# First tokens normed tile by tile, last counts between additions, and a graph convolution's matrix scaled a tile ahead

## What is computed

```python
xn = _layernorm(x)
x = x + _L0_gnn_ref(xn, W1, b1, W2, b2, edge_index) + _L0_mix_ref(xn[None], w_map, ...)[0]
# _L0_gnn: twice gcn_conv, A = D^-1/2 (counts of edges + identity) D^-1/2, deg = row sums
#   h = relu(A (xn W1) + b1);  out = A (h W2) + b2
# _L0_mix: linear attention: k, v = layernorm per head (12 heads of 64), att = k^T v / n, out = (q att) w_out
```

## Time and profile before

| | us |
|---|---|
| median of three runs | 2002.79 |
| the profiled execution, its own time | 2000.80 |
| its span, first to last instruction | 1998.9 |
| PE busy | 1862.9 (93%) |
| DVE busy | 1292.3 (65%) |
| ACT busy | 934.8 (47%) |

### The profile page before, as it was taken

The page is one execution under the profiler, slowest core; times in us unless marked ns, Lnnn a source line. Parts: engine busy times, 40 slices in busy tenths (PEclk is TensorE's granted clock), DMA queues, the critical chain, the costliest instruction groups (busy, mean ns, idle before and its releaser), DMA issues.

```text
span 1998.9 us, 30899 instructions
## 1 busy us (share of the span) xinstructions
PE 1862.9 (93%) x12197; PEld 1769.2 (89%) x12198; DVE 1292.3 (65%) x2466; ACT 934.8 (47%) x1543; POOL 154.5 (8%) x129
## 2 busy tenths in 40 slices
PE   5997998899999999788679999999999999999998
PEld 4885788899889999788679999999999999999998
DVE  6997766545345646888873764356565666676886
ACT  2321222324233535878543233336555666666775
POOL 0000000004000003333110000000101001001010
PEclk8997999999999989899889999999999999999999
DMA  3110002101122211110212132255656657676795
GB/s 116 48 48 1 24 25 97 38 24 49 48 72 88 72 38 46 69 38 17 95 51 87 49 103 72 71 187 194 206 202 212 216 213 239 232 259 233 286 327 195
DMA packets 36796, 234.30 MB, mean 117 GB/s; under 512 B 5916, under 2 KB 7318, under 8 KB 14632
## 3 DMA queue, kind: packets, MB, share of 16 engines
q1 hardware_dynamic: 31318, 217.41, 30.4%
q0 software_dynamic: 2656, 8.99, 2.0%
q10 hardware_dynamic: 2674, 5.87, 0.8%
HBM read 221.91 MB, written 10.35 MB: 116 GB/s over the span
## 4 chain that ended last, share of the span: by engine, by line
PE 45%; issue 6%; DVE 3%; ACT 2%; DMA 1%; POOL 0%; ACTq 0%; POOLq 0%; DVEq 0%
PE bank L2682 8%; PE bank L341 7%; PE bank L342 7%; PE bank L343 7%; PE bank L2683 3%; PE bank L2694 3%; PE bank L2698 2%; PE bank L2686 2%; PE bank L2695 2%; PE bank L2697 1%; PE bank L2685 1%; DVE weight_lo L314 1%; PE bank L2643 0%; PE bank L2032 0%; DMA weight_raw_fifth<-in_ffn_w 0%
## 5 line engine op out<-in xcount | busy, mean ns | idle before, releaser
L314 DVE TENSOR_TENSOR weight_lo<-weight_raw,weight_hi 128x2304 fp32r<-128x2304 f32 (+1 forms) x155 | 392.3, 2535 | 46.1 <-ACT weight_hi L304 45.9
L304 ACT ACTIVATE weight_hi<-weight_raw 128x2304 fp32r<-128x2304 f32 (+1 forms) x155 | 323.2, 2087 | 71.4 <-DMA weight_raw<-in_ffn_w 50.8
L341 PE MATMUL bank<-xT_hi,weight_hi 128*128 128x320 f32 (+1 forms) x576 | 182.6, 317 | 1.9 <-DVE xT_lo L362 1.8
L342 PE MATMUL bank<-xT_lo,weight_hi 128*128 128x320 f32 (+1 forms) x576 | 177.8, 309 | 0.0
L343 PE MATMUL bank<-xT_hi,weight_lo 128*128 128x320 f32 (+1 forms) x576 | 177.6, 308 | 0.0
L341 PE MATMUL bank<-weight_hi,xT_hi 128*128 128x384 f32 (+1 forms) x480 | 161.9, 337 | 7.9 <-DVE xT_lo L362 4.5
L3056 DVE TENSOR_TENSOR hidden_tmp<-hidden_tmp,bank 128x160 f32<-128x160 f32 (+5 forms) x192 | 65.7, 342 | 159.1 <-ACT hidden_tmp L2842 159.1
L342 PE MATMUL bank<-weight_lo,xT_hi 128*128 128x384 f32 (+1 forms) x480 | 157.5, 328 | 0.0
L343 PE MATMUL bank<-weight_hi,xT_lo 128*128 128x384 f32 (+1 forms) x480 | 157.3, 328 | 0.0
L665 PE MATMUL bank<-one_hot_dst,one_hot_src 125*128 125x313 f16 x800 | 122.9, 305 | 15.2 <-ACT packed_counts L679 7.9
L2842 ACT ACTIVATE hidden_tmp<-bank,ffn_b_by_load 128x160 f32<-128x160 f32 (+5 forms) x192 | 73.6, 404 | 121.0 <-PE bank L2686 118.8
(11 more groups left out here) (499 smaller groups left out, 5078.9 us busy)
## 6 DMA issues: line engine op xcount, KB each, us to landing
weight_raw<-in_ffn_w SPq DMA_DIRECT2D x111, 1152.0 KB, 5.2
weight_raw_fifth<-in_ffn_w SPq DMA_DIRECT2D x25, 1152.0 KB, 5.3
weight_raw<-in_shared_w SPq DMA_DIRECT2D x16, 1152.0 KB, 5.1
weight_raw<-in_mix_kv SPq DMA_DIRECT2D x8, 1152.0 KB, 5.2
weight_raw<-in_gat_w SPq DMA_DIRECT2D x8, 768.0 KB, 4.2
weight_raw<-in_mix_q SPq DMA_DIRECT2D x4, 1152.0 KB, 5.0
weight_raw<-in_mix_out SPq DMA_DIRECT2D x4, 1152.0 KB
weight_raw<-in_gnn_w SPq DMA_DIRECT2D x4, 1152.0 KB, 5.1
```

What stands on the lines that cost most here:

```text
L304: act.activation(upper_, whole_, ACT.Copy).then_inc(*w_hi.one())
L314: dve.tensor_tensor(lower_, whole_, upper_.bitcast(F32), ALU.subtract).then_inc(*w_lo.one())
L341: pe.matmul(dst, a[0], b[0], start=first, stop=False)
L342: pe.matmul(dst, a[0], b[1], start=False, stop=False)
```

## The change

The first norm uses `tile_norm`: x comes in tiles, each with a semaphore of its own, with weight 0 and the edges between tiles 1 and 2. Tiles 0 and 1 are normed before the first product, tiles 2 to 4 between the first keys' products and the first columns; weight 1 is split after tile 4. In `project(1)` each of the last four unpacking steps follows an addition, and weight 8 is split before `project(1)`. In the graph convolution tile t + 1 is scaled before `adj_lo` of tile t. The hooks `scalar_meanwhile` and `vector_meanwhile` of `layer_norm` go away.

```diff
-        sp.dma_start(x[:, 0:TT - 1, :], ins["x"][0:(TT - 1) * P, :]...).then_inc(*x_in.dma())
-        sp.wait_ge(blank.semaphore, 1)
-        for a0, n in parts_of_16(LAST):
-            sp.dma_start(x[a0:a0 + n, TT - 1, :], ...).then_inc(*x_in.dma())
+        def tile(t):
+            sp.dma_start(x[:, t, :], ins["x"][t * P:(t + 1) * P, :]).then_inc(*x_in[t].dma())
+        tile(0)
+        tile(1)
+        weights_load(1)
         for n, name in enumerate(("src", "dst")):
             for a0, rows in parts_of_16(EP):
                 sp.dma_start(edges_i[a0:a0 + rows, n, :], ins[name][a0:a0 + rows, :]).then_inc(*edges_in_.dma())
+        tile(2)
+        tile(3)
+        sp.wait_ge(blank.semaphore, 1)
+        for a0, n in parts_of_16(LAST):
+            sp.dma_start(x[a0:a0 + n, TT - 1, :], ...).then_inc(*x_in[TT - 1].dma())
         weights_load(DEPTH - 1)
...
             def keys_or_values(n, beside):
                 w = weight("mix0_kv", n)
                 for t in range(TT):
+                    if n == 0:
+                        if 2 <= t + 1 < TT:
+                            norm.turn_tensor(t + 1)
+                        pe.wait_ge(*norm.ready[t])
                     bank = ring.next(kv_copied.at(TT * n + t + 1))
...
-            pe.wait_ge(*xT_ready)
+            pe.wait_ge(constants.semaphore, 2)
+            norm.turn_tensor(0)
+            norm.turn_tensor(1)
             keys_or_values(0, FIRST)
...
+        def moments_of(t):
+            dve.wait_ge(*x_in[t].now())
+            norm.stats_vector(t)
+        def first_vector_steps():
+            moments_of(0)
+            norm.scale_vector(0)
+            moments_of(1)
+            norm.scale_vector(1)
+            norm.lower_vector(0)
+            norm.lower_vector(1)
+            dve.memset(zeros[:, :, :], 0.0).then_inc(*pads_blank.one())
+            edges_ready()
+            return dve_own.now()
...
+            norm.root_scalar(0)
+            norm.root_scalar(1)
+            norm.upper_scalar(0)
+            norm.upper_scalar(1)
+            weight_hi(0)
+            norm.root_scalar(2)
+            norm.upper_scalar(2)
+            act.wait_ge(*edges_read)
+            act.wait_ge(*constants.now())
             for t in range(TT):
                 copied(0, t)
                 edges_scalar(FIRST[t])
+                if 3 <= t + 3 < TT:
+                    norm.root_scalar(t + 3)
+                    norm.upper_scalar(t + 3)
+                if t == 2:
+                    weight_hi(1)
...
                         dve.tensor_tensor(x[:, t, cols], x[:, t, cols], out_banks[n][:, 0:HALF], ALU.add).then_inc(*out_added.one())
-                    if i == 1 and c == 0:
-                        for step in range(4):
-                            unpack(CHUNKS - 1, step)
-            dve.memset(zeros[:, :, :], 0.0).then_inc(*pads_blank.one())
-            edges_vector(sum(FIRST) + AHEAD)
+                        if i == 1 and c == 0 and t < 4:
+                            unpack(CHUNKS - 1, t)
+            edges_vector(2)
+            weight_lo(0)
+            ahead = 2
+            for t in range(2, TT):
+                moments_of(t)
+                edges_vector(2)
+                norm.scale_vector(t)
+                edges_vector(FIRST[t - 2] - 2)
+                norm.lower_vector(t)
+                ahead += FIRST[t - 2]
+            edges_vector(2)
+            weight_lo(1)
+            edges_vector(sum(FIRST) + AHEAD - ahead - 2)
...
+                if n == PAIRS - 1:
+                    weights_lo(c0 + 6)
                 if n % 3 == 2:
                     project(n // 3, PROJECTION if n == 2 else 0)
-            weights_lo(c0 + 6)
             weights_lo(c0 + 7)
...
             for t in range(TT):
-                dve.scalar_tensor_tensor(loops[:, t, :], loops[:, t, :], deg_col[:, t:t + 1], deg_row[:, :],
-                                         ALU.mult, ALU.mult).then_inc(*looped.one())
+                for i in (0, 1) if t == 0 else [t + 1] if t + 1 < TT else []:
+                    dve.scalar_tensor_tensor(loops[:, i, :], loops[:, i, :], deg_col[:, i:i + 1], deg_row[:, :],
+                                             ALU.mult, ALU.mult).then_inc(*looped.one())
                 dve.wait_ge(*adj_hi.at(1 + t + 1))
                 lower(at(adj, ALL, t, ALL), loops[:, t, :]).then_inc(*adj_lo.one())
```

More of the change, by code:

```diff
@@ L384, in program @@
     constants, ones_made = sig("constants_made"), sig("ones_made")
-    x_in, edges_in_ = sig("x_landed"), sig("edges_landed")
+    x_in, edges_in_ = [sig("x_landed0"), sig("x_landed1")] + [sig("x_landed")] * (TT - 2), sig("edges_landed")
     blank = sig("blank_made")
@@ L407, in first_sync @@
     def first_sync():
-        sp.dma_start(x[:, 0:TT - 1, :], ins["x"][0:(TT - 1) * P, :].rearrange("(t p) d -> p t d", p=P)).then_inc(*x_in.dma())
-        sp.wait_ge(blank.semaphore, 1)
-        for a0, n in parts_of_16(LAST):
-            sp.dma_start(x[a0:a0 + n, TT - 1, :], ins["x"][(TT - 1) * P + a0:(TT - 1) * P + a0 + n, :]).then_inc(*x_in.dma())
+        def tile(t):
[3 more added lines that the diff above has]
+        weights_load(1)
         for n, name in enumerate(("src", "dst")):
@@ L414, in first_sync @@
                 sp.dma_start(edges_i[a0:a0 + rows, n, :], ins[name][a0:a0 + rows, :]).then_inc(*edges_in_.dma())
+        tile(2)
+        tile(3)
+        sp.wait_ge(blank.semaphore, 1)
+        for a0, n in parts_of_16(LAST):
+            sp.dma_start(x[a0:a0 + n, TT - 1, :], ins["x"][(TT - 1) * P + a0:(TT - 1) * P + a0 + n, :]).then_inc(*x_in[TT - 1].dma())
         weights_load(DEPTH - 1)
@@ L424, in program, with layer_norm @@
     first_scalar()
-    def layer_norm(xn, *x_ready, scalar_meanwhile=None, vector_meanwhile=None):
+    def layer_norm(xn, *x_ready):
         var, std, normed, turned, xT_hi, xT_lo = sigs("ln_variance", "ln_deviation", "ln_normed", "xT_turned", "xT_hi", "xT_lo")
@@ L446, in vector @@
                                   ALU.subtract, ALU.mult).then_inc(*normed.one())
-            if vector_meanwhile:
-                vector_meanwhile()
             for t in range(TT):
@@ L456, in scalar @@
             act.activation(rstd[:, :], rstd[:, :], ACT.Sqrt).then_inc(*std.one())
-            if scalar_meanwhile:
-                scalar_meanwhile()
             for t in range(TT):
@@ L963, in vector @@
                     weights_lo(c0 + 5)
+                if n == PAIRS - 1:
+                    weights_lo(c0 + 6)
                 if n % 3 == 2:
                     project(n // 3, PROJECTION if n == 2 else 0)
-            weights_lo(c0 + 6)
             weights_lo(c0 + 7)
[L969 to L980, removed]
         ring.banks, ring.until, ring.k = psum[0:3], ring.until[0:3], 0
+        norm = tile_norm(xn)
+        xT_ready = norm.ready[-1]
         tensor()
+        edges_read = first_vector_steps()
         scalar()
```

## The result

The changed kernel takes 1982.14 us, the median of four runs (1980.26 to 1982.57), where the kernel before, run beside it, takes 2001.90 (2000.47 to 2003.74, four runs). The ratio is 0.9898, with a 95% interval of 0.9884 to 0.9912: faster, by 19.8 us. The forecast was 1989.5, between the 1988.3 and 1990.3 that its sum of 12.5 gives, with 1983.5 as the low end of the range. So the sign was right, and the time came out 7.4 us under the forecast and 1.4 us under the range. The two profiled executions differ by 20.5, where the sum had 12.5.

A forecast was written before the change was run, and what follows sets the result against it. TensorE, busy 93%, bounds the kernel, with VectorE as full between 60 and 190. Terms -3.9 - 3.15 - 2.9 - 2.6 = -12.5 gave 1988.3 from the profiled 2000.8, 1990.3 from the median 2002.8; stated 1989.5, range 1983.5 to 1996.5.

The forecast's parts named there:

- The start: First norm and first keys: first product at 17.2 instead of 28.59, part given back; -3.9 us, ends -1 and -8.
- The three bank waits: First keys: product t waits for ScalarE to copy the bank of product t - 1; 1.1 us, three times, 3.3.
- TensorE turns three tiles, 3 x 1.2 = 3.6: First keys: transposes of tiles 2 to 4 now lie between products, giving back 3.6 us at 1.2 a tile.
- VectorE ... ends the reduction of tile 4 not 4.5 but about 3.9 early: End of the first keys: VectorE, which paces the next stretch, gains about 3.9 us where TensorE gains 4.5.
- The hand-over: Last projection to graph convolution: 2.1 of new waits for 1.91 removed, weight 8 already split; -3.15 us, bounds 0 and -4.
- The scaling: Graph convolution before A h: scaling a tile ahead leaves about 1.15 of the 4.09 us gap; -2.9, bounds 2.0 and 3.3.
- The clock behind it: Behind the scaling's gap: no clock fall expected, winning 2.6 of the 2.7 us lost at 1.2 GHz; bounds 0 and -2.7.
- rival D: More won: no bank waits (-3.3), fewer 1.2 GHz stretches behind 120 (up to 5); -17.5, 1984.5 us; chance 0.12.
- B: First keys: new waits, 2.4 a tile instead of 1.1, take the start's term to 0; -8.6, 1993.4 us; chance 0.14.
- C: Hand-over: late additions hold TensorE for all they free, the wait only moves; -9.35, 1992.7 us; chance 0.08.
- E: First keys: gaps in each tile keep TensorE at 1.2 GHz, 20 to 24 us more; slower, 2011.5 us; chance 0.04.
- F: Whole kernel: no gain, B and C together with a clock that falls anyway; 1999.1 us; chance 0.04.

The follow-up runs named there:

- e9: The changed kernel run once more, with nothing altered; 1979.80 us, ratio 0.9887 to the kernel before.
- e1: The kernel before with only the first norm by tiles, with its loads, columns and the split of weight 1 behind tile 4; 1993.75 us, ratio 0.9958.
- e4: The kernel before with only the split of weight 8 moved ahead of the last projection; 1999.93 us, ratio 0.9991.
- e5: The kernel before with only the four last unpacking steps spread behind four additions; 1995.21 us, ratio 0.9974.
- e3: The kernel before with only the scaling done a tile ahead; 1996.47 us, ratio 0.9964.
- e12: e6 with one more edit: weight 8 is split behind the eighth addition of `project(1)`; 1977.14 us, ratio 0.9881 to the kernel before.
- e14: The same kernel as e12, run in another batch; 1977.16 us, ratio 0.9882 to the kernel before.
- e6: The changed kernel with ScalarE copying product t before making the upper part of tile t + 2; 1980.01 us, beside 1979.80 for the changed kernel.

## Why the prediction was right and wrong

**The start, -3.9: the mechanism right, the size wrong; -6.6 measured.** The three bank waits came out at 1.11 for 1.1 and the first product at 16.65 for 17.2. The main step that failed here is "TensorE turns three tiles, 3 x 1.2 = 3.6". The 1.2 came from the 24 transposes of the earlier trace rows, which ran ahead of the clock's rise; between products a turn takes 0.82. The table gives 12.5 - 6.55 = 5.95 for three turns with three waits of 1.11, so 2.6 for the turns: 1.0 of the miss. The first product was 0.55 earlier than worked out, as tile 0 released VectorE at 4.00 and not at 4.8. The clock rose 3.0 us behind it (at 19.6), where before it took 4.4: 12.5 - 11.94, another 0.55. This part is luck: in e9 it took 5.8, and the same kernel's start is worth 5.65. And the step "VectorE ... ends the reduction of tile 4 not 4.5 but about 3.9 early" is wrong: in after VectorE's reduction of tile 4 is 6.1 earlier, and by before's 84 it is 6.6 earlier, as TensorE is: 0.6. These four make 2.7. e1, with 6.2 at the same place, says the same without the other edits.

**The hand-over, -3.15: right to 0.4; -3.5 measured** (21.39 less 17.92), with waits of 0.79 and 0.42 for the forecast 1.0, 0.5 and 0.6. Its account holds: new waits stand in the projection for the old one, and the 3.16 behind it is won. e4 and e5 show both halves at work, with idle time down by 1.6 and by 1.9.

**The scaling, -2.9: right; -3.0 measured,** with 1.17 left of the gap for the forecast 1.15, and rounds of 2.0 for 2.1. **The clock behind it, -2.6: right; -2.7 measured** (15.78 - 13.05), in e3 alone 2.7.

**The sum.** The four terms measure 6.6 + 3.5 + 3.0 + 2.7 = 15.8 where the prediction had 12.5; of the miss of 3.3, 2.7 are in the start. Another 4.8 of the profiled difference is the clock behind 720, for which the sum had no term: this is the second step that failed. It stood only in rival D, as "fewer stretches at 1.2 GHz behind 120", with a chance of 0.12. D's price for it ("up to 5") was right; its place was not, as the stretch at 190 is there in after too, at 183, and neither did the bank waits go. D's own sum is short as well: its two parts, 3.3 and 5, on top of 12.5 make 20.8 and not 17.5, which is 1981.2 by the same reckoning, and 1982.14 was measured. With D at 1984.5 the range ended at 1983.5; it had room for a start that is 3 better or for a fall less, and both came. The Trainium skill, "TensorE: Matmul & The Clock Gate", in its part on the gate, was cited for shifted work meeting or missing a fall either way; with the gaps of 0.74 alike in both kernels and e12 and e14 falling out differently, the traces here are in keeping with it.

**What the runs do not settle** is how often each kernel meets the fall. Single runs have a time and a mean granted clock over the whole span, and neither tells this fall from others; the low stretches between 800 and 1000 differ from profile to profile as well. Of the seven profiles without all three edits five have the fall, of the seven with all three one. That points to the change, but it is too few to show it, and e12 and e14 show that chance has a part. So of the 19.8 us, some 15.8 are shown stage by stage, up to 1 of them by the luck of the clock's rise; that another 4.8 are the clock is shown for the two profiled executions, and some of it is lost again behind 800; that the change made the fall rarer is not shown.

**The rivals.** B (the start eaten by the new waits) is refuted by e1, and e6 shows how little the waits are worth. C (the wait moves to the additions) is refuted by the gaps of 0.79 and 0.42. E (slower), the clock down through the first keys, did not come: from 19.68 on equal matmuls stand 0.18 apart. F fell with B and C.

## What to carry to other kernels

Cost a short operation from a row at the clock that it will run at: a transpose timed ahead of the clock's rise was a third too dear. When an edit seems to earn nothing, add up the idle time and look at the clock of its stage before calling it useless: the split of weight 8 alone took 1.6 us of waits away and one low stretch of the clock hid it. And compare two traces by the shift of the same instructions, stage by stage, before believing a few microseconds of the total: nearly 5 of these 20 came from a stretch that nobody edited.

## What was not expected of the hardware

Ahead of the first change that the record holds, the granted clock stands at 1.00 though TensorE runs slower. TensorE's timeline and windows of after, at the first product:

```profile
17.78 0.52 PE L341 MATMUL bank<-weight_hi,xT_hi 128*128 128x384 f32 x1
...
18.74 0.52 PE L341 MATMUL bank<-weight_hi,xT_hi 128*128 128x384 f32 x1
...
19.68 0.34 PE L341 MATMUL bank<-weight_hi,xT_hi 128*128 128x384 f32 x1
...
20.21 0.34 PE L341 MATMUL bank<-weight_hi,xT_hi 128*128 128x384 f32 x1
```

```profile
18.00:19.00 1.00, 1.00 (x4) 1.00 (x4) 1.00 (x4) 0.19 (x1) 0.00 (x0) 1.00 0.16 40
```

Between two of these rows lie three matmuls: 0.96 / 3 = 0.32 us each up to 18.74, and 0.53 / 3 = 0.18 behind 19.68, with 1.00 printed in the window of the slow ones. The spacing of equal matmuls shows the clock where the column does not.

The second is the price of the fall itself. Two executions of one kernel, e12 and e14, differ in a stretch of 10.2 us at 1.2 GHz with the same work and the same idle time ahead of it. It costs 4.8 us between them, and 4.8 between before and after. That is more than the hand-over earned (3.5), and nearly what the scaling earned together with the clock behind it (5.7).
